# The column scan of a four-layer convolution kernel: the bias of the candidate n moves from VectorE's sum into ScalarE's tanh, and the matmuls for z stand ahead of those for n

## The reference, cut to what matters

```python
def _cell(prev_col, cur_col, weight_ih, bias_ih, weight_hh, bias_hh):
    pad = jnp.pad(prev_col, ((0, 0), (1, 1), (0, 0)))
    x = jnp.concatenate([pad[:, :-2], pad[:, 1:-1], pad[:, 2:]], axis=-1)
    i_vals = jnp.einsum('bhk,ok->bho', x, weight_ih) + bias_ih
    h_vals = jnp.einsum('bhc,oc->bho', cur_col, weight_hh) + bias_hh
    r_i, z_i, n_i = jnp.split(i_vals, 3, axis=-1)
    r_h, z_h, n_h = jnp.split(h_vals, 3, axis=-1)
    r = jax.nn.sigmoid(r_i + r_h)
    z = jax.nn.sigmoid(z_i + z_h)
    n = jnp.tanh(n_i + r * n_h)
    return n * z + cur_col * (1.0 - z)
```

## Time and profile before

| what | value |
|---|---|
| median of 3 runs | 597.79 us (596.89 to 597.91) |
| the profiled execution: its own time | 597.76 us |
| its span in the trace | 595.9 us |
| scan, from the first L1344 to the last | 117.5 to 321.0 us |
| DVE busy in the whole span | 492.0 us (83%) |
| ACT busy | 396.7 us (67%) |
| PE busy | 539.8 us (91%) |
| POOL busy | 311.3 us (52%) |

### The profile page before, as it was taken

How to read it: one execution, slowest core, us unless ns; L and a number is a source line. 1 busy time by engine, 2 the same in 40 slices (tenths; PEclk the granted TensorE clock), 3 DMA queues, 4 the chain that set the end, 5 groups by cost and what they waited for, 6 DMA issues and landing times.

```text
span 595.9 us, 26842 instructions
## 1 busy us (share of the span) xinstructions
PE 539.8 (91%) x10404; PEld 429.0 (72%) x10404; DVE 492.0 (83%) x1273; ACT 396.7 (67%) x897; POOL 311.3 (52%) x425
## 2 busy tenths in 40 slices
PE   3999999699999999999999999988889778999996
PEld 2333333477777777777777999987577667899995
DVE  7778977479989898989898787798899999377876
ACT  3445879767777776777778966676378966756441
POOL 7665654156666666666665302035799799121000
PEclk9999999899999999999999999999999997999999
DMA  6900000011111111111113100003158775003324
GB/s 226 383 6 0 2 2 4 14 39 44 40 40 44 38 41 44 36 44 40 40 44 103 50 2 0 0 2 85 60 151 248 213 227 158 31 1 142 141 123 159
DMA packets 21284, 45.69 MB, mean 77 GB/s; under 512 B 5104, under 2 KB 15600, under 8 KB 20352
## 3 DMA queue, kind: packets, MB, share of 16 engines
q1 hardware_dynamic: 20160, 44.97, 24.2%
q10 hardware_dynamic: 672, 0.15, 0.1%
q0 software_dynamic: 416, 0.07, 0.1%
HBM read 28.53 MB, written 8.39 MB: 62 GB/s over the span
## 4 chain that ended last, share of the span: by engine, by line
DVE 40%; PE 36%; issue 14%; ACT 6%; DVEq 2%; DMA 1%; SPq 0%; ACTq 0%
PE psum L655 8%; DVE spec L1352 8%; DVE work L338 7%; DVE spec L1344 6%; DVE spec L1355 5%; PE psum L770 5%; PE psum L909 5%; PE psum L925 5%; PE psum L786 4%; DVE small L1237 3%; PE psum L898 3%; PE psum L754 2%; ACT work L295 2%; PE psum L828 2%; DVE spec L1347 2%
## 5 line engine op out<-in xcount | busy, mean ns | idle before, releaser
L690 PE MATMUL psum<-spec,matrices 128*32 128x128 f32 x3024 | 110.0, 279 | 14.4 <-ACT spec L1016 7.5
L690 PEld LDWEIGHTS psum<-spec,matrices 128*32 128x32 f32 x3024 | 76.5, 110 | 46.6 <-ACT spec L1016 46.5
L531 POOL TENSOR_TENSOR spec<-spec 64x128 f32<-64x128 f32 x126 | 70.6, 560 | 72.1 <-DVE spec L1355 72.1
L697 PE MATMUL psum<-spec,matrices 128*32 128x128 f32 x3024 | 107.4, 274 | 0.7 <-DMA spec<-work 0.6
L697 PEld LDWEIGHTS psum<-spec,matrices 128*32 128x32 f32 x3024 | 85.6, 111 | 3.7 <-issue 3.6
L828 PE MATMUL psum<-work 128*32 128x128 f32 x2368 | 74.8, 281 | 14.8 <-ACT work L350 10.2
L655 PE MATMUL psum<-spec,matrices 128*64 128x512 f32 x384 | 86.4, 607 | 1.1 <-ACT spec L950 1.1
L828 PEld LDWEIGHTS psum<-work 128*32 128x32 f32 x2368 | 65.7, 113 | 23.7 <-issue 22.2
L338 DVE TENSOR_TENSOR work<-spec,psum 32x512 f32<-32x512 f32 x108 | 73.5, 681 | 3.8 <-PE psum L828 0.5
L509 POOL TENSOR_SCALAR spec<-image,small 32x960 f32<-32x960 f32 (+1 forms) x48 | 55.5, 1157 | 34.6 <-PE psum L655 22.0
L525 POOL TENSOR_TENSOR image<-image,spec 128x128 f32 (+1 forms) x128 | 69.4, 542 | 0.0
(11 more groups left out here) (154 smaller groups left out, 935.5 us busy)
## 6 DMA issues: line engine op xcount, KB each, us to landing
work<-w_dram SPq DMA_DIRECT2D x33, 512.0 KB, 4.2
spec<-work SPq DMA_DIRECT2D x124, 64.0 KB, 1.9
image<-x_dram SPq DMA_DIRECT2D x3, 2048.0 KB, 11.7
out_dram<-image SPq DMA_DIRECT2D x3, 2048.0 KB, 6.3
image<-x_dram SPq DMA_DIRECT2D x4, 512.0 KB, 5.8
work<-w_dram SPq DMA_DIRECT2D x1, 2048.0 KB, 7.7
out_dram<-image SPq DMA_DIRECT2D x4, 512.0 KB, 2.9
kept<-const_dram SPq DMA_DIRECT2D x1, 192.0 KB, 5.5
```

The lines of the kernel that those rows point to most:

```text
L531: nc.gpsimd.tensor_tensor(straddled(h, ROWS_01, 0), *of, ALU.subtract).then_inc(lower_ready[h], 1)
L690: last = mm(psum[QUARTERS[hm], 4 * h + g, 0:HB], sv[:, g, QUARTERS[hm]], moving[hm], start=starts, stop=True)
L697: last = mm(psum[q, 4 * h + g, 0:HB], sv[:, 3 + g, q], e, start=True, stop=stops)
```

## The change

Three edits. PE does the 4 matmuls for z ahead of those for n. The tanh takes the bias of n as its own bias operand. DVE's L1347 loses that operand and becomes a plain sum of two tensors. The two lines become one, so that later DVE lines carry numbers lower by one (L1352 is L1351, L1355 is L1354, L1360 is L1359).

```diff
                 from_state(h, 0).then_inc(r_sum[h], 1)
+                from_state(h, 1).then_inc(z_sum[h], 1)
                 from_state(h, 2, True).then_inc(n_sum[h], 1)
-                from_state(h, 1).then_inc(z_sum[h], 1)
...
             def candidate(h, w):
                 act.wait_ge(pre_ready[h], w)
-                a(gn[h], pre2[h], ACT.Tanh).then_inc(n_gate[h], 1)
+                a(gn[h], pre2[h], ACT.Tanh, bias=bias_s[:, 2:3]).then_inc(n_gate[h], 1)
...
                 dve.wait_ge(n_sum[h], w)
-                v.scalar_tensor_tensor(out=pre2[h], in0=psum[:, 4 * h + 2, 0:HB], scalar=bias_s[:, 2:3], in1=pre1[h],
-                                       op0=ALU.add, op1=ALU.add).then_inc(pre_ready[h], 1)
+                v.tensor_tensor(pre2[h], pre1[h], psum[:, 4 * h + 2, 0:HB], ALU.add).then_inc(pre_ready[h], 1)
```

## The result

The changed kernel is slower: 600.07 us in the median of 6 runs, beside 597.58 us of the kernel before in 6 runs. The ratio is 1.0041, with a 95% interval of 1.0024 to 1.0057. The profiled execution took 599.7 us with a span of 597.9, beside a span of 595.9 before.

A forecast was written before the change was run, and what follows sets the result against it. The prediction took a closed ring over DVE and ACT's tanh as the bound: 126 half-steps x (92 - 71 = 21 ns) = 2.6 us more, less 0.2 at the start, gives 600.2 us, 0.4% slower; range 597.4 to 602.4.

The forecast's parts named there:

- The ring over DVE and the tanh: Closed cycle of L1344, L1347, the tanh, L1355 and L1360; claimed to set the pace without slack, 1.55 us a half-step.
- PE's long wait for L1016: PE's 42.4 us wait for ACT's edge copy in the scan; claimed not to show that PE and ACT set the pace.
- The column costs the tanh 92 ns: ACT's tanh in each half-step, 282 ns without a bias column; claimed 92 ns longer with one, bounds 0 and 105.
- The plain sum saves 71 ns: DVE's L1347 in each half-step; claimed to fall from 351 to 280 ns, as L1344 has the same form.
- the case in which the prices cancel: Rival: column costs 61 to 82 ns, or part of the longer tanh hides; 596.6 to 599.0 us, 12%.
- The start gains 0.2: Second half-step of the scan: z about 0.4 us earlier, n 0.2 late; a gain of 0.2 us, once.
- z first costs and gives nothing in the steady state: PE's new order; claimed to shorten a ring over ACT and PE that isn't the bound, so costed at nothing.
- n isn't late there: L1347's wait for n: ready 0.93 us after PE's start, wanted at 1.12 earliest; the late-n rival, 612 us, had 3%.
- The keep product is the next bound: DVE's L1352, hidden beside the tanh; claimed to let L1355 begin no sooner than 0.66 us after L1347's start.
- The rival of a column that costs nothing: Rival: the tanh's column costs nothing or little, gaining 5 to 9 us over the scan, about 591 us; 13%.
- the ring over ACT and PE: Second cycle, L1016, PE's matmuls and L1025; claimed 1.59 us a half-step, 1.47 with z first, and not the bound.

The follow-up runs named there:

- the order alone: Kernel before with one edit, PE's matmuls for z ahead of those for n, the bias staying in DVE's sum: 597.28 us, ratio 1.0008.
- the kernel with zeros: Kernel before with a bias column of zeros given to the tanh, the sum keeping its own column: 608.28 us, ratio 1.0191.
- without a bias: Changed kernel with the bias of n_i left out of the computation, z ahead of n: 589.71 us, ratio 0.9879.
- POOL's add later: Changed kernel with no bias for n_i, and POOL's L525 waiting for the other half's keep product: 610.63 us, ratio 1.0226 to the kernel before.

## Why the prediction was right

The kernel was forecast at 600.2 us, and 600.07 was measured: right in the direction, the mechanism and the size. That it is right to 0.13 us is luck. With both prices as they were measured, the prediction's own sum would have been 3.4 - 0.2 = 3.2 us, thus 601.0; the profile after gave back 1.0 us behind the scan, with the clock, which the prediction had not counted.

- *The ring over DVE and the tanh bounds the scan.* Shown. A column in the tanh alone lengthens each half-step by its full 90 ns, and the same column on both engines adds up. Taking it away from both shortens the scan, until the next link.
- *PE's long wait for L1016 means nothing.* Shown by the order alone, which shortens that ring and moves nothing. How much it shortens it was mis-sized, at 0.12 us (1.59 to 1.47). From PE's start to L1025 it was 0.93 before and is 0.70 now (301.62 to 302.32), so 0.23 less and a ring of 1.36, because L1025 follows the start of L1021 by 0.20 and not by 0.31. It made no difference, since the ring isn't the bound in either case.
- *The column costs the tanh 92 ns.* It was 90; the little square roots and the big normalisations of the earlier trace rows had been good rows to price it by, although neither is a tanh or writes to PSUM. The idle time ahead of the tanh doesn't hide it: it took 371 ns or more in all 126 half-steps of the kernel with zeros. By the second figure of the Trainium skill's page "ScalarE: Activation LUTs" (about 280 ns + 0.833 ns for each element, in "What ACT_TABLE_LOAD costs") the tanh would have taken an estimated 387 ns; the trace has 372, and the measurement decides.
- *The plain sum saves 71 ns.* This term was mis-sized: it saved 63. I took L1344's 280 ns for the form, and L1347 takes 288. The net is thus 27 ns instead of 21, 3.4 us instead of 2.6. Why two instructions of one form differ by 8 ns wasn't tried. The lower end of the case in which the prices cancel, 596.6, also leaves out the 0.2 us of the start that the forecast has; it doesn't touch the verdict.
- *The start gains 0.2.* The first two gaps went from 2.90 and 2.03 to 2.89 and 1.88, a gain of 0.16, in two profiles whose clock rose at the same 120.90 us. The links were the forecast ones: L1025 began at 120.44 instead of 120.94, and L1347 waited for n and began at 120.93 instead of 120.72. In other profiles the clock decides how long the start takes. 3.4 less 0.2 is 3.2, and the scan grew by 3.0.
- *z first costs and gives nothing in the steady state, and n isn't late there.* Shown: one wait of 0.3 us for n in the whole scan, in the second half-step.
- *The keep product is the next bound, at 0.66 after L1347.* Shown without a bias: L1354 began 0.67 after it (226.32 to 226.99), and 0.63 when the keep product was no longer stretched. The rival of a column that costs nothing was priced at 5 to 9 us by this, and the scan without a bias is 6.5 us shorter.
- *In that case the ring over ACT and PE would come in with the old order, and not with the new.* Right: 4.6 us between the two orders without a bias. The link was the tanh behind L1016, which the prediction didn't name.

## What to carry to other kernels

Find the closed ring of instructions that sets the pace, and price an edit only by the links that lie on it; the largest wait in the profile may belong to a ring that merely follows. Moving an operand from one engine to the next within the same ring saves nothing by itself: what counts is what each engine asks for it, here 63 ns on VectorE and 90 on ScalarE. An edit worth nothing may be worth 4 us as soon as its neighbour is gone, so it should be tried again after each change of the bound.

## What was not expected of the hardware

- POOL's L525 stretches a DVE instruction with two SBUF tensors that begins while L525 runs: the keep product from 280 to 530 ns (465 in the kernel before, where it begins later), the state's difference from 290 to 480. In all four kernels looked at (before, changed, no bias with z first, POOL's add later) it ends 0.14 to 0.15 us after L525 does, in the median, so it comes through only when L525 is done. DVE instructions with one operand in PSUM aren't stretched: L1347 keeps its 351 to 353 ns in the kernel before also in the 20 half-steps in which L525 began first.
- The rows speak for which of the two begins first, and not for the stride of L525's column. The state's difference begins ahead of POOL's L531 in every half-step, and takes its 0.29. The start of the kernel with POOL's add later has three exceptions from the usual pairs. Twice the state's difference began ahead of L525; it took 0.29, and L525 took 0.70 in place of 0.56. Once the keep product began behind L531, which reads two tiles without a stride; it took 0.53 and ended 0.15 after L531. These are few cases, and no run was made for them. The first and the last of the three:

```profile
126.17 0.29 DVE L1361 TENSOR_TENSOR spec<-spec 128x128 f32<-128x128 f32 x1
126.18 0.70 POOL L525 TENSOR_TENSOR image<-image,spec 128x128 f32 x1 [1.00 <-DVE spec L1353]
...
126.82 0.44 POOL L531 TENSOR_TENSOR spec<-spec 64x128 f32<-64x128 f32 x1
126.89 0.53 DVE L1353 SCALAR_TENSOR_TENSOR spec<-spec,work 128x128 f32<-128x128 f32 x1
```

- A turn of DVE's loop costs 0.38 us in which nothing is waited for, and 14 fewer turns gave 4.8 us of scan. PE turns too, and its weight loads of L697 sat idle 15 times, 3.8 us in all, with nothing to wait for; that isn't on DVE's ring.
